# Attention in a two-layer fp32 model: two PSUM banks for the transposed probabilities, four places for their copies, the products with values a step later, and the sums in two full banks

## The chip, the core and the metric

One core of a Trainium2 chip runs the whole program. The metric is device time in microseconds (us), the median of three timed executions. The engines are PE (TensorE, the matrix engine, with its weight loads as PEld), DVE (VectorE), ACT (ScalarE), POOL (GpSimd) and SP, the engine that issues most DMAs. They run their own instruction streams and wait for one another through semaphores. Matrix products land in PSUM, eight banks of 512 fp32 columns on 128 partitions.

## The reference

The model maps x (64 batch elements, 32 tokens, 512 features) through two layers. The first is a state-space convolution along the tokens and a feed-forward with low-rank experts; the second is attention over a paged cache and such a feed-forward again. The change lies in the attention:

```python
q, k, v = x @ Wq.T, x @ Wk.T, x @ Wv.T          # 32 query heads, 8 key heads, D = 128
q, k = rope(rmsnorm(q)), rope(rmsnorm(k))
k_all = concat([k_cache[block_table], k])        # 512 cached keys + 32 own
v_all = concat([v_cache[block_table], v])
scores = where(valid, q @ k_all.T / sqrt(128), -1e30)
o = softmax(scores) @ v_all                      # 4 query heads share one key head
return o @ Wo.T
```

Each batch element has 16 cached pages of 32 keys. The 32 tokens of the 4 query heads that share a key head make 128 rows, so one unit of work is one key head of one element: 128 rows of scores over 544 keys. There are 64 x 8 = 512 units.

## The kernel before

`attention` (line 974) is a software pipeline written out by hand. `turns` (line 671) makes one loop step for each unit and calls `step` with a predicate `live(k)`: the work under `live(k)` in step u belongs to unit u - k. Each engine has its own `step` and runs its parts in the order in which they are written. One turn of the loop is 16 steps, two batch elements; a group is four units, the half of an element that fills a set of sums.

On PE, a step holds:

- under `live(4)` (line 1122) the scores: six fp32r matmuls of 272 columns, two for each of three split products. They go into banks 0 to 3 in turn.
- under `live(6)` (line 1131) four transposes of the probabilities `pr` into the one bank `ps_w` (bank 4). They wait for `s_e` (ACT has made these probabilities) and for `s_pt >= m` (ACT has copied the unit before out of the bank).
- once for each group, under `live(7)` (lines 1139 and 1141), the transposes of the probabilities of the own keys (`pr_new`) and, every second group, of the reciprocal sums `ri`. They go into the right half of bank 5 or 7.
- under `live(7)` (line 1156) four matmuls with values: `v_raw` times `pt`, ACT's copy of the transposed probabilities. They wait for `s_pt`, at k == 2 also for `s_o`, at k == 0 for `s_wn`. `pt` has two places.
- once for each group, under `live(8)` (line 1164), four matmuls for the own values, each over 64 of the 128 partitions. `v_new` is block-diagonal with zeros elsewhere: head k has its 32 rows at partitions 32k to 32k + 31.

ACT copies the finished sums to `ot` (lines 1248 to 1252), copies `ps_w` to `pt` (line 1260), copies `pt_new` and `rt`, takes the exponentials with their sums (line 1273), and once an element rounds the queries (line 1278). DVE splits the keys into a high part (line 1202) and a low part (line 1205), adds the mask and takes the row maxima (line 1212), and splits the queries (line 1226).

What sets the loads: when PE has ended the second group's own values of element b (`s_nw`), POOL copies the next row numbers (line 1086) and gathers the values of b + 2 by four indirect DMAs (line 1080). SP at the same signal loads the own values of b + 2 (line 1038), stores element b (lines 1044 and 1046), and then issues the queries (line 1019) and the 17 key loads (lines 1030 and 1033) of b + 3. DVE's first key split of an element (line 1202 at g == 0) waits for all 17.

Names used below: the step of an element counts 0 to 7 by PE's loop, j mod 8. Step 0 comes directly behind line 1164 of an element's second group in the kernel before, so POOL's copy falls at the start of step 0. The first key split is in DVE's step 2; its low part, in step 3, is needed by the scores of step 4.

## Time and profile before

| | |
|---|---|
| median of 3 runs | 2556.46 us (2554.64 to 2559.14) |
| profiled execution | 2546.38 us, span 2544.5 us |
| PE busy | 2437.2 us, 96% of the span |
| DVE, ACT, POOL busy | 1890.9, 1315.4, 764.1 us |
| attention | about 825 to 2080 us of the span |
| DMA | 213 GB/s over the span |

A line of the timeline gives the start, the time from first start to last end of a run of equal instructions, the engine, the line of the kernel and what is written from what. An fp32 matmul stands there as two records, a transpose as one. In brackets stands the idle time before it and what ended it. The end of a matmul is modelled and overlaps the next one, so the starts are the thing to compare. "Remote" as the releaser means that the profile ties the end of the wait to no instruction of this core.

### The profile page before, as it was taken

Reading aid. Unit: us, or ns where it says so; the run is one execution under the profiler, and the core shown is the slowest. Engines: PE = TensorE matmul, PEld = TensorE weight load, DVE = VectorE, ACT = ScalarE, POOL = GpSimd, SP = SyncE. Lnnn points to the kernel's source line nnn. Section 1 sums busy time; section 2 is a strip of 40 time slices with the busy share of each in tenths; the row PEclk is TensorE's granted clock in tenths of the full one; section 3 lists DMA queues with packets and bytes.
Section 4 is the critical chain, followed back from the end, with each engine's and each line's share of the span. In section 5 each row is a group of like instructions: output and inputs, shape, how many; then the busy total and the mean of one; then the engine's idle time right before and its main releaser. Section 6 shows DMA issues by size and latency. Waiting matters only on the chain. (4 is left out here: it accounts for less than half of the span.)

```text
span 2544.5 us, 54152 instructions
## 1 busy us (share of the span) xinstructions
PE 2437.2 (96%) x16128; PEld 2136.9 (84%) x16128; DVE 1890.9 (74%) x3300; ACT 1315.4 (52%) x3824; POOL 764.1 (30%) x740
## 2 busy tenths in 40 slices
PE   5999999999989999999999999999999989999999
PEld 4777877787767899999999999999999977777767
DVE  7568999999951777777777777777777766566652
ACT  2325555555532667666667666666666651111120
POOL 0235666666631122222222222222222221131120
PEclk8999999999999999999999999999999999999999
DMA  8623333333346688888888888878888886756512
GB/s 313 236 88 98 96 95 95 95 111 95 95 139 205 219 287 271 284 296 276 272 289 291 275 279 291 288 268 280 292 289 273 286 265 218 231 188 221 186 49 99
DMA packets 434116, 542.35 MB, mean 213 GB/s; under 512 B 36980, under 2 KB 350100, under 8 KB 429460
## 3 DMA queue, kind: packets, MB, share of 16 engines
q1 hardware_dynamic: 391012, 394.37, 46.6%
q0 software_dynamic: 36864, 134.23, 16.1%
q10 hardware_dynamic: 6192, 13.13, 1.5%
q8 instruction: 28, 0.46, 0.1%
q14 instruction: 20, 0.16, 0.0%
HBM read 440.59 MB, written 101.01 MB: 213 GB/s over the span
## 5 line engine op out<-in xcount | busy, mean ns | idle before, releaser
L1212 DVE CUSTOM_DVE_ANT_0 at_sm<-ps,at_mask 128x544 f32<-128x544 f32 x512 | 369.1, 721 | 297.4 <-PE ps L1122 199.9
L1156 PE MATMUL ps<-at_pt,at_v_raw 128*128 128x128 f32 x4096 | 542.0, 275 | 2.8 <-issue 2.8
L1156 PEld LDWEIGHTS ps<-at_pt,at_v_raw 128*128 128x128 f32 x4096 | 498.5, 192 | 3.0 <-issue 3.0
L1260 ACT ACTIVATE at_pt<-ps 128x512 f32<-128x512 f32 x512 | 304.1, 594 | 324.7 <-PE ps L1131 215.9
L1273 ACT ACTIVATE at_pr<-at_sm,at_nm 128x544 f32<-128x544 f32 x512 | 382.9, 748 | 59.7 <-DVE at_nm L1212 48.2
L895 POOL TENSOR_TENSOR pr_m<-pr_qn,tb 128x256 f32<-128x256 f32 x320 | 331.9, 1057 | 250.6 <-DVE pr_qn L864 235.5
L1131 PE MATMUL ps<-constants,at_pr 128*128 128x128 f32 x2048 | 310.7, 274 | 33.0 <-ACT at_pt L1260 31.0
L732 PE MATMUL ps<-pr_hi,xh 128*128 (+1 forms) x768 | 318.4, 415 | 7.9 <-DVE pr_qn L864 5.5
L1205 DVE TENSOR_TENSOR at_k_lo<-shared,at_k_hi 128x1088 fp32r<-128x1088 f32 x256 | 325.8, 1273 | 0.0
L1080 POOL DMA_INDIRECT at_v_raw<-v_cache,at_idx x256 | 287.1, 1122 | 113.4 <-issue 62.6
L733 PE MATMUL ps<-pr_lo,xh 128*128 (+1 forms) x768 | 305.1, 397 | 0.0
L734 PE MATMUL ps<-pr_hi,xl 128*128 (+1 forms) x768 | 303.5, 395 | 0.0
L822 ACT ACTIVATE pr_sq<-ps 128x128 f32<-128x128 f32 x640 | 168.5, 278 | 226.9 <-DVE f_a L857 223.8
L1086 POOL COPY at_idx<-at_rows 128x4 uint32 (+1 forms) x64 | 11.9, 186 | 901.4 <-PE ps L1164 823.7
L1131 PEld LDWEIGHTS ps<-constants,at_pr 128*128 128x128 f32 x2048 | 238.6, 141 | 49.3 <-issue 25.9
L1122 PE MATMUL ps<-at_k_hi,at_q_hi 128*128 128x272 f32 x1024 | 257.6, 333 | 2.1 <-ACT pr_stage L846 2.1
L1415 PE MATMUL ps<-op_o_hi,op_w_hi 128*128 128x512 f32 x512 | 205.6, 402 | 8.2 <-DVE op_o_lo L1380 8.2
L1122 PE MATMUL ps<-at_k_hi,at_q_lo 128*128 128x272 f32 x1024 | 212.6, 289 | 0.0
L1122 PE MATMUL ps<-at_k_lo,at_q_hi 128*128 128x272 f32 x1024 | 211.6, 288 | 0.0
L1364 ACT ACTIVATE op_o_hi<-o_raw 128x2048 fp32r<-128x2048 f32 x32 | 61.2, 1915 | 288.7 <-PE ps L1417 288.7
L1417 PE MATMUL ps<-op_o_hi,op_w_lo 128*128 128x512 f32 x512 | 205.5, 401 | 0.0
L1416 PE MATMUL ps<-op_o_lo,op_w_hi 128*128 128x512 f32 x512 | 204.8, 400 | 0.0
(237 smaller groups left out, 4374.5 us busy)
## 6 DMA issues: line engine op xcount, KB each, us to landing
shared<-k_t SPq DMA_DIRECT2D x1024, 128.0 KB
qk_t<-pr_stage SPq DMA_DIRECT2D x160, 256.0 KB
shared<-qk_t SPq DMA_DIRECT2D x64, 512.0 KB, 7.6
o_t<-at_ot SPq DMA_DIRECT2D x64, 512.0 KB
o_raw<-o_t SPq DMA_DIRECT2D x32, 1024.0 KB, 6.0
shared<-ri_d SPq DMA_DIRECT2D x32, 1024.0 KB, 8.1
f_w<-wqkv SPq DMA_DIRECT2D x12, 1024.0 KB, 6.1
s_k_in<-k_cache SPq DMA_DIRECT2D x16, 512.0 KB, 7.4
```

The lines of the kernel that those rows point to most:

```text
L732: e.matmul(out, xh[:, k, cols], hi, start=(k == 0), stop=False)
L733: e.matmul(out, xh[:, k, cols], lo, start=False, stop=False)
L734: last = e.matmul(out, xl[:, k, cols], hi, start=False, stop=(k == KB - 1))
L895: ins = e.tensor_tensor(heads(m2[:, q, :])[:, :, a], heads(qn[:, q, :])[:, :, b], table(tb, i, j - 3, a), ALU.mult)
L1080: e.indirect_dma_start(out=v_raw[:, q, c, :], out_offset=None, in_=dram["v_cache"], in_offset=bass.IndirectOffsetOnAxis(ap=idx[:, q, c:c + ...
L1122: last = e.matmul(ps[:, 2 * r + h, 0:W], a[:, q, mine], b[:, w, g % 2, h * W:(h + 1) * W], start=first, stop=end)
L1131: last = e.transpose(ps_w[:, c * P:(c + 1) * P], pr[:, w, k, c * P:(c + 1) * P], ident)
L1156: last = e.matmul(sums(w, k), v_raw[:, q, c, g * D:(g + 1) * D], pt[:, r, c * P:(c + 1) * P], start=(k % 2 == 0 and c == 0), stop=False, s ...
L1205: e.tensor_tensor(two(k_lo), raw, two(k_hi).bitcast(F32), ALU.subtract).then_inc(s_lo, 1)
L1212: e.tensor_tensor_reduce(out=halves(sm[:, r, :]), in0=ps[:, 2 * r:2 * r + 2, 0:W], in1=halves(mask[:, q, :]), scale=-SC, scalar=3e38, op0= ...
L1260: e.activation(pt[:, r, :], ps_w, ACT.Copy).then_inc(s_pt, 1)
L1273: e.activation(pr[:, w, k, :], sm[:, r, :], ACT.Exp, bias=nm[:, at], scale=-1.0, accum_out=su[:, at]).then_inc(s_e, 1)
```

## The change

The transposed probabilities go to bank 4 and bank 7 in turn, and the transposes wait for the copy of the unit before the last (`s_pt >= m - 1`). `pt` has four places and lies in another part of SBUF. The products with values come under `live(8)`, one step later; the own values under `live(9)`, the copy of the sums under `live(10)`. The four sums of a group take one full bank, 5 or 6; the transposed `pr_new` and `ri` go into the bank of the other group's sums, before these begin, and wait for `s_o` there. The own values are four matmuls over all 128 partitions, with one signal in place of two. The sums of each group are copied by one activation. The lead of the loop is 12 steps in place of 11.

```diff
         place("gap2", [P, 256])
-        self.pt = place("pt", [P, 2, LK])
+        place("gap4", [P, 2 * LK])
         place("gap3", [P, 32])
...
+        pt = sb("pt", [P, 4, LK])
...
-        ps_w = ps[:, 4, :]
-        turned = lambda w: ps[:, 7 - 2 * w, 2 * P:4 * P]
-        sums = lambda w, k: ps[:, 6 if k >= 2 else 5 + 2 * w, k % 2 * P:(k % 2 + 1) * P]
-
-        steps = lambda e, step: turns(e, B * UB, PER, 11, step)
+        ps_w = lambda r: ps[:, 4 + 3 * r, :]
+        turned = lambda w: ps[:, 6 - w, 0:2 * P]
+        sums = lambda w, k: ps[:, 5 + w, k * P:(k + 1) * P]
+
+        steps = lambda e, step: turns(e, B * UB, PER, 12, step)
...
-                    e.wait_ge(s_nw, (b + 1) * 4)
+                    e.wait_ge(s_nw, (b + 1) * 2)
                     load_v(b + 2, q)
                     store(b, q)
...
-                    wait_apart(e, s_passed[0], (s_nw, (b + 1) * 4))
+                    wait_apart(e, s_passed[0], (s_nw, (b + 1) * 2))
                     indices(b + 2, q)
...
                     e.wait_ge(s_e, m + 1)
-                    wait(e, s_pt, m)
+                    wait(e, s_pt, m - 1)
                     for c in range(KC):
-                        last = e.transpose(ps_w[:, c * P:(c + 1) * P], pr[:, w, k, c * P:(c + 1) * P], ident)
+                        last = e.transpose(ps_w(jj % 2)[:, c * P:(c + 1) * P], pr[:, w, k, c * P:(c + 1) * P], ident)
                     last.then_inc(s_c, 1)
                 if live(7) and (j - 7) % QU == QU - 1:
                     jj = j - 7
                     w = (jj // QU) % 2
                     n = jj // QU
+                    e.wait_ge(s_o, i * 4 + n + 1)
                     if w == 1:
...
-                if live(7):
-                    m, jj = u - 7, j - 7
-                    g, q, r, k, w = jj % UB, (jj // UB) % 2, jj % 2, jj % QU, (jj // QU) % 2
+                if live(8):
+                    m, jj = u - 8, j - 8
+                    g, q, k, w = jj % UB, (jj // UB) % 2, jj % QU, (jj // QU) % 2
...
-                    if k == 2:
-                        e.wait_ge(s_o, i * 4 + jj // QU + 1)
                     e.wait_ge(s_pt, m + 1)
                     for c in range(KC):
-                        last = e.matmul(sums(w, k), v_raw[:, q, c, g * D:(g + 1) * D], pt[:, r, c * P:(c + 1) * P],
-                                        start=(k % 2 == 0 and c == 0), stop=False, skip_group_check=True)
-                if live(8) and (j - 8) % QU == QU - 1:
-                    jj = j - 8
+                        e.matmul(sums(w, k), v_raw[:, q, c, g * D:(g + 1) * D], pt[:, jj % 4, c * P:(c + 1) * P],
+                                 start=(k == 0 and c == 0), stop=False, skip_group_check=True)
+                if live(9) and (j - 9) % QU == QU - 1:
+                    jj = j - 9
                     g, q, w = jj % UB, (jj // UB) % 2, (jj // QU) % 2
                     e.wait_ge(s_wn, i * 4 + jj // QU + 1)
-                    for k in (0, 2, 1, 3):
-                        rows = slice(k // 2 * 2 * S, (k // 2 + 1) * 2 * S)
-                        last = e.matmul(sums(w, k), v_new[rows, q, g // QU, k * D:(k + 1) * D], pt_new[rows, w, :],
-                                        start=False, stop=(k % 2 == 1), skip_group_check=True)
-                        if k % 2 == 1:
-                            last.then_inc(s_nw, 1)
+                    for k in range(QU):
+                        last = e.matmul(sums(w, k), v_new[:, q, g // QU, k * D:(k + 1) * D], pt_new[:, w, :],
+                                        start=False, stop=(k == QU - 1), skip_group_check=True)
+                    last.then_inc(s_nw, 1)
...
-                if live(9) and (j - 9) % QU == QU - 1:
-                    jj = j - 9
+                if live(10) and (j - 10) % QU == QU - 1:
+                    jj = j - 10
...
-                    e.wait_ge(s_nw, i * 8 + jj // QU * 2 + 2)
-                    if t == 0:
-                        e.activation(ot[:, q, 0:4 * P].rearrange("p (a x) -> p a x", a=2), ps[:, 5:7, 0:2 * P],
-                                     ACT.Copy).then_inc(s_o, 1)
-                    else:
-                        e.activation(ot[:, q, 6 * P:8 * P], ps[:, 6, 0:2 * P], ACT.Copy)
-                        e.activation(ot[:, q, 4 * P:6 * P], ps[:, 7, 0:2 * P], ACT.Copy).then_inc(s_o, 1)
+                    e.wait_ge(s_nw, i * 4 + jj // QU + 1)
+                    e.activation(ot[:, q, t * QU * P:(t + 1) * QU * P], ps[:, 5 + t, :], ACT.Copy).then_inc(s_o, 1)
...
                     e.wait_ge(s_c, m + 1)
-                    e.activation(pt[:, r, :], ps_w, ACT.Copy).then_inc(s_pt, 1)
+                    e.activation(pt[:, jj % 4, :], ps_w(jj % 2), ACT.Copy).then_inc(s_pt, 1)
```


PE in the loop, from the transposes of a step 3 on. The names are those of the code: `at_pt,at_v_raw` are products with values, `at_pt_new,at_v_new` the own values. Before:

```order
L1131 MATMUL ps<-constants,at_pr 128x128 x4
L1156 MATMUL ps<-at_pt,at_v_raw 128x128 x4
L1164 MATMUL ps<-at_pt_new,at_v_new 128x128 x4
L1115 REGISTER_ALU
L1117 REGISTER_ALU
L660 REGISTER_ALU
L1122 MATMUL ps<-at_k_hi,at_q_hi 128x272 x2
L1122 MATMUL ps<-at_k_lo,at_q_hi 128x272 x2
L1122 MATMUL ps<-at_k_hi,at_q_lo 128x272 x2
L1131 MATMUL ps<-constants,at_pr 128x128 x4
L1156 MATMUL ps<-at_pt,at_v_raw 128x128 x4
```

PE at the same place in the changed kernel, where lines 1123, 1132 and 1163 are the scores, the transposes and the own values:

```order
L1132 MATMUL ps<-constants,at_pr 128x128 x4
L1156 MATMUL ps<-at_pt,at_v_raw 128x128 x4
L1116 REGISTER_ALU
L1118 REGISTER_ALU
L660 REGISTER_ALU
L1123 MATMUL ps<-at_k_hi,at_q_hi 128x272 x2
L1123 MATMUL ps<-at_k_lo,at_q_hi 128x272 x2
L1123 MATMUL ps<-at_k_hi,at_q_lo 128x272 x2
L1132 MATMUL ps<-constants,at_pr 128x128 x4
L1156 MATMUL ps<-at_pt,at_v_raw 128x128 x4
L1163 MATMUL ps<-at_pt_new,at_v_new 128x128 x4
```

The own values have moved from the end of steps 3 and 7 to the end of steps 4 and 0, behind the next scores, transposes and products.

ACT at the turn from one element to the next, before. Here `at_ot` is the copy of the sums, `at_pt` that of the transposed probabilities, `at_pr` the exponentials and `at_q_hi` the rounded queries:

```order
L1251 ACTIVATE at_ot<-ps 128x256
L1252 ACTIVATE at_ot<-ps 128x256
L1260 ACTIVATE at_pt<-ps 128x512
L1272 REGISTER_ALU
L1273 ACTIVATE at_pr,at_su<-at_sm,at_nm 128x544
L1277 ISA
L1278 ACTIVATE at_q_hi<-shared 128x1024
L1260 ACTIVATE at_pt<-ps 128x512
```

ACT at the same place in the changed kernel:

```order
L1253 ACTIVATE at_pt<-ps 128x512
L1265 REGISTER_ALU
L1266 ACTIVATE at_pr,at_su<-at_sm,at_nm 128x544
L1270 ISA
L1271 ACTIVATE at_q_hi<-shared 128x1024
L1245 ACTIVATE at_ot<-ps 128x512
L1253 ACTIVATE at_pt<-ps 128x512
```

The copy of the sums is one activation, and it stands behind the rounding of the queries instead of ahead of the step's copy. DVE, POOL and SP have the same instructions in the same order inside the steps; the signal `s_nw` that POOL and SP wait for comes one step later.

## Rows read from the trace of the kernel before

**Rows 1.** Busy time of each engine in attention, with granted clock and DMA:

```profile
core 0: us, PE busy (x) PEld busy (x) DVE busy (x) ACT busy (x) POOL busy (x), PEclk, DMA share, GB/s
825.00:2080.00 1255.00, 1215.38 (x10434) 1166.01 (x10432) 963.86 (x1981) 857.96 (x1986) 291.64 (x311) 1.00 0.84 279
```

**Rows 2.** Who waited for whom: PE, 860 to 2080 us (total, times, longest):

```profile
PE ps L1131 <- ACT at_pt L1260: 31.0, 52, 0.7
PE ps L1131 <- issue: 2.0, 3, 0.7
```

**Rows 3.** PE in order of time, steps 2 to 5 of one element:

```profile
start us, us, engine line op out<-in xcount [idle before <-releaser]
1407.17 0.60 PE L1131 MATMUL ps<-constants,at_pr 128*128 128x128 f32 x4
...
1408.53 0.50 PE L1122 MATMUL ps<-at_k_hi,at_q_hi 128*128 128x272 f32 x2
...
1410.16 0.63 PE L1131 MATMUL ps<-constants,at_pr 128*128 128x128 f32 x4 [0.63 <-ACT at_pt L1260]
1410.62 1.06 PE L1156 MATMUL ps<-at_pt,at_v_raw 128*128 128x128 f32 x8
1411.61 0.72 PE L1164 MATMUL ps<-at_pt_new,at_v_new 64*128 64x128 f32 x8
1412.25 0.52 PE L1122 MATMUL ps<-at_k_hi,at_q_hi 128*128 128x272 f32 x2
...
1413.11 0.60 PE L1131 MATMUL ps<-constants,at_pr 128*128 128x128 f32 x4
1413.55 1.06 PE L1156 MATMUL ps<-at_pt,at_v_raw 128*128 128x128 f32 x8
1414.36 0.50 PE L1122 MATMUL ps<-at_k_hi,at_q_hi 128*128 128x272 f32 x2
```

**Rows 4.** ACT, step 2 of that element, and steps 2 and 3 two elements before:

```profile
1369.48 0.60 ACT L1260 ACTIVATE at_pt<-ps 128x512 f32<-128x512 f32 x1 [0.65 <-issue]
...
1372.72 0.60 ACT L1260 ACTIVATE at_pt<-ps 128x512 f32<-128x512 f32 x1 [1.75 <-PE ps L1131]
...
1409.41 0.60 ACT L1260 ACTIVATE at_pt<-ps 128x512 f32<-128x512 f32 x1 [2.25 <-remote]
```

**Rows 5.** DVE, step 2 and the low parts of the keys in step 3:

```profile
1408.88 0.72 DVE L1212 CUSTOM_DVE_ANT_0 at_sm<-ps,at_mask 128x544 f32<-128x544 f32 x1 [1.96 <-PE ps L1122]
...
1410.13 1.28 DVE L1205 TENSOR_TENSOR at_k_lo<-shared,at_k_hi 128x1088 fp32r<-128x1088 f32 x1
```

**Rows 6.** POOL: copies of row numbers, and one late gather:

```profile
857.33 0.18 POOL L1086 COPY at_idx<-at_rows 128x4 uint32 x1 [30.16 <-PE ps L1164]
...
1364.20 0.18 POOL L1086 COPY at_idx<-at_rows 128x4 uint32 x1 [13.25 <-PE ps L1164]
...
1368.40 0.95 POOL L1080 DMA_INDIRECT at_v_raw<-v_cache,at_idx  x1 [2.24 <-issue]
...
1382.86 0.18 POOL L1086 COPY at_idx<-at_rows 128x4 uint32 x1 [10.28 <-PE ps L1164]
...
1402.53 0.18 POOL L1086 COPY at_idx<-at_rows 128x4 uint32 x1 [13.28 <-PE ps L1164]
...
1422.01 0.19 POOL L1086 COPY at_idx<-at_rows 128x4 uint32 x1 [13.12 <-PE ps L1164]
...
2045.01 0.18 POOL L1086 COPY at_idx<-at_rows 128x4 uint32 x1 [13.09 <-PE ps L1164]
```

**Rows 7.** The stretches in which DMA runs dry (columns as rows 1):

```profile
1421.00:1422.00 1.00, 1.00 (x11) 0.87 (x11) 0.51 (x1) 0.92 (x3) 0.00 (x0) 1.00 0.07 21
...
1441.00:1442.00 1.00, 1.00 (x12) 0.88 (x9) 0.09 (x1) 0.92 (x4) 0.19 (x1) 1.00 0.33 114
```

**Rows 8.** DVE, the first key split of the next element but one:

```profile
1445.20 0.79 DVE L1202 CAST at_k_hi<-shared 128x1088 fp32r<-128x1088 f32 x1
```

**Rows 9.** PE, the first products with values:

```profile
835.99 2.05 PE L1156 MATMUL ps<-at_pt,at_v_raw 128*128 128x128 f32 x8 [2.81 <-issue]
```

More of the change, by code:

```diff
@@ L995, in attention @@
         v_raw, v_new, k_hi, k_lo, q_hi, q_lo, ot = early.v_raw, early.v_new, early.k_hi, early.k_lo, early.q_hi, early.q_lo, early.ot
-        pt, pr_new, nm, su, ri, s_in, s_qhi = early.pt, early.pr_new, early.nm, early.su, early.ri, early.s_in, early.s_qhi
+        pr_new, nm, su, ri, s_in, s_qhi = early.pr_new, early.nm, early.su, early.ri, early.s_in, early.s_qhi
         sm = sb("sm", [P, 2, NKEY])
         pr = sb("pr", [P, 2, QU, NKEY])
+        pt = sb("pt", [P, 4, LK])
         pt_new = sb("pt_new", [P, 2, P])
```

## The prediction, written before the changed kernel ran

> **What bounds the kernel now.** The first view is the busy time of attention: from 825 to 2080 us PE is busy for 1215 of 1255 us at a granted clock of 1.00, that is 2.4 GHz, DVE for 964 and ACT for 858 [rows 1]. PE sets the time there, and only what PE does or waits for counts. The second view is the waits of PE: 55 waits in this stretch, all ahead of the transposes of line 1131, 52 of them for ACT's copy `at_pt`, 0.7 us at the longest [rows 2]. The third is the timeline of PE around one of them. In step 3 the scores start at 1408.53 and the transposes at 1410.16, 1.63 us later; in step 4 the same distance is 0.86 (1412.25 to 1413.11) [rows 3]. With the slower restart (0.46 against 0.44 from the transposes to the products) a wait costs about 0.8 us.
>
> Why is the copy late? The transposes of step 2 start at 1407.17 and take 0.60, but ACT begins their copy only at 1409.41, after 2.25 us of idleness that the profile puts down to "remote" [rows 3, 4]. DVE, too, begins the maxima of step 2 at 1408.88, though their scores were done before 1407.6 [rows 5]. So once in most elements the news from PE reaches both readers about 1.7 us late. With one bank the next transposes cannot go on without that copy, and PE pays what its own 2.1 us step (1412.25 to 1414.36) does not cover.
>
> The lateness goes with the gathers. The element whose row numbers POOL copied at 1364.20 had its second gather late, at 1368.40 after 2.24 us of idleness [rows 6]; there ACT's copy of step 2 was on time (1369.48) and that of step 3 was the late one (1372.72, idle 1.75) [rows 4]. PE lost nothing: the next POOL copy came 18.66 us later (1382.86), where the mean of the 61 periods from 857.33 to 2045.01 is 19.47 [rows 6]. This element is nearly the experiment: everything that hangs on the gathers moved by about 1.9 us against PE's scores.
>
> **The change part by part.**
>
> *Two banks and one step more.* The transposes of a step now need the copy made two steps before, and the products with values use a copy that is a step older. A copy that starts 1.7 us late is then covered twice over. All 55 waits go as far as this copy is their cause. Their worth is the distance of the mean period from the clean one, 19.47 - 18.66 = 0.81 us for each of 62 periods, 50 us in all; 55 waits at 0.8 give 44, and the rest is the transposes of step 2 that start late without counting as idle. I take the first, since it is read from ends of periods.
>
> *What is late next.* The signal `s_nw` now comes behind step 0, so POOL's gathers and SP's loads move 2.1 us later against the scores. The late news (6.35 to 6.9 us after POOL's copy of 1402.53 [rows 4 to 6]) then falls on step 3. ACT has its slack. DVE begins the maxima of step 3 up to 1.8 us late and must still do a mask, a high part, the maxima of step 4 and a low part of 1.28 [rows 5] before the scores of step 6. Counting these up from 7.2 us after the copy I get 11.15 where PE wants to start at 11.0: 0.15 us in perhaps every second element. I charge 0.08 a period, 5 us in all; the bounds are 0 and, if also signals to PE are held back, 0.9 a period (the second rival).
>
> *Own values over 128 partitions.* Before, PE goes from the products at 1410.62 to the own values at 1411.61 and to the scores at 1412.25, where products without own values take 0.81 (1413.55 to 1414.36) [rows 3]. So the own values cost 0.18 before their first matmul and 0.64 for eight records, 0.82. The new ones have the shape of the products, eight records in 0.81. I take no change; the bounds are no change and +0.18 for each of 128 groups, 23 us, if the gap ahead of them is not due to their shape. The Trainium skill speaks on both sides here (TensorEngine Tiling (Array Packing), Key Properties and Theoretical Speedup): a change of tiling mode drains the engine, and two tiles of 64 rows work in parallel, up to twice as fast. By the second rule alone the pairs would take half of 0.81, and giving them up would cost 0.4 us a group, 51 us. The trace has 0.64 plus a gap of 0.18 that fits the drain: the rule's gain is nearly absent and what is left of it pays for the drain.
>
> *The copies of the sums.* One activation of 512 columns each time; ACT idles for a third of attention [rows 1] and the sums are now needed a step later, so nothing. The new wait `s_o` ahead of the transposed `pr_new` asks for a copy that ACT begins a step earlier, about 2 us ahead. Behind that wait stand the products and the next scores, so if ACT were more than 2 us behind, PE would wait here instead.
>
> *Keys and values.* They are requested 2.1 us later against the scores. DMA ran dry at about 1421.1 and 1441.4, 18.6 and 19.4 us after the POOL copies at 1402.53 and 1422.01, and the key split that needs the second batch came at 1445.20, 23.2 after its copy [rows 6 to 8]. In the new order the split comes at 23.2 - 2.1 - 0.7 (the shorter period) = 20.4. That leaves 1.0 us at the tighter element, so I charge nothing. If the cover goes, see the third rival.
>
> *Both ends.* The first products wait 2.81 us for their values at 836 us [rows 9]. One step of scores and transposes now stands ahead of them and can fill about 1 us of it: -1. The last group gets one step more to drain, whose work is the same: 0.
>
> The sum: -50 + 5 - 1 = -46 us. The profiled execution took 2546.4 (span 2544.5), which would become 2500. The three timed runs have a median of 2556.5, 10 us above it, and I carry the same saving over: **2510 us**.
>
> **Rivals.**
>
> *The gap ahead of the own values stays.* The gap of 0.18 could belong to the wait for `s_wn` that the first of these matmuls carries, not to its shape. Against it: the copy was made more than a step before. Then +23 us: 2533.
>
> *Signals to PE are held back as well.* The rows show only news from PE arriving late. If news from DVE is held too, the low part of the keys decides. It ends at about 5.4 us after POOL's copy in the new order and the scores of step 4 want to start at 6.0, where the old order gave them 0.8 more, since the own values stood between steps 3 and 4. Held until 6.9 they stall PE by 0.9 a period, as much as before: 62 x (0.81 - 0.9) = +6 us, 2562. If it hits every second element: 2535. For it: DVE's low part is the tightest supply of PE. Against it: in the shifted element nothing stalled, though there the scores of step 4 came 0.8 later.
>
> *Keys arrive late (the slower side).* SP and DMA become the bound if the 17 key loads of an element end more than about 22.5 us after POOL's copy; the split has 1.0 us to spare at 19.4, and DVE and PE together have about 2 more. They would be 3 us later than now, for example because the store and the gathers collide with the next element's loads. Each us beyond costs one us a period: at 23.0, 0.5 us of loss on the old period, 62 x 0.5 = +31, 2587. For it: a DMA share of 0.84 over attention [rows 1]. Against it: the queues run dry in every element now, for about 2 us.
>
> *The change does not do what it says:* PE's waits have the same count under another name, for example behind `s_o` or `s_e` because ACT itself is late with the exponentials. Then no change, 2556. ACT's 858 of 1255 us speaks against it.
>
> **How the numbers follow.** My forecast has 0.66, with its own range 2503 to 2518: the upper saving is 50 + 4, the lower one leaves 0.15 more a period. The gap that stays has 0.07, held signals 0.14 (two thirds of it in the milder form, still faster), late keys 0.05, no effect 0.04; 0.04 is for things that I don't see, half of them faster. Faster by over 0.2% (5 us, about what a measurement tells from nothing): 0.66 + 0.07 + 0.09 + 0.02 = 0.84. Within 0.2%: 0.08. Slower: 0.08. The range 2502 to 2537 takes in the staying gap and the milder form of held signals and leaves out about 0.18.
>
> **What would show it.** Right: no idle time of PE ahead of the transposes, POOL copies 18.7 to 18.8 us apart, ACT's late copy now in step 3 and still late, eight records of own values in about 0.81 with no gap ahead, DMA running dry less than 20.4 us after POOL's copy. Wrong: waits of PE ahead of the scores with DVE's low part as releaser (the second rival), DVE idle ahead of the first key split (the third), or a gap of 0.18 still ahead of the own values (the first). If the late news does not move with POOL's gathers but stays where it was, my account of its cause is wrong, even if the time is right: the two banks would still cover ACT, but DVE's low part in step 3 would end at 1411.41 where the scores now come at about 1410.6, and the gain would shrink to near nothing.

## The result

The changed kernel took 2522.53 us (median of 4 runs, 2520.02 to 2523.79) beside 2556.62 us of the kernel before on the same chip (4 runs, 2554.64 to 2559.14): a ratio of 0.9865, 95% interval 0.9853 to 0.9878. That is 34 us saved where 46 were forecast. The profiled execution of the changed kernel took 2522.86 us (span 2521.0), 23.5 less than the profiled one of before, which had been 10 us faster than its own timed runs.

The experiments fell on four chips, and on three of them the gain is absent: the kernel before takes 2498 us there, the changed one 2504 on the one chip of the three where it ran (chip 9), and its variants on the other two 2503 to 2505. So what has to be explained is both where the gain came from and why it comes on some chips only.

### The profile page after: what moved, and what is told of

Read it like the earlier page. It is cut to its first block and busy times, and to the rows that moved or that the text cites. A ratio compares the mean times of both kernels' runs of the same rounds, so it can differ in the third digit from the quotient of the medians.

```text
span 2521.0 us, 54056 instructions
## 1 busy us (share of the span) xinstructions
PE 2444.8 (97%) x16128; PEld 2178.7 (86%) x16128; DVE 1894.9 (75%) x3300; ACT 1312.9 (52%) x3760; POOL 756.2 (30%) x740
## 5 line engine op out<-in xcount | busy, mean ns | idle before, releaser
L1210 DVE CUSTOM_DVE_ANT_0 at_sm<-ps,at_mask 128x544 f32<-128x544 f32 x512 | 369.3, 721 | 264.8 <-PE ps L1123 252.8
L1156 PE MATMUL ps<-at_pt,at_v_raw 128*128 128x128 f32 x4096 | 540.9, 275 | 0.0
L1156 PEld LDWEIGHTS ps<-at_pt,at_v_raw 128*128 128x128 f32 x4096 | 497.8, 192 | 0.0
L1253 ACT ACTIVATE at_pt<-ps 128x512 f32<-128x512 f32 x512 | 304.2, 594 | 299.9 <-PE ps L1132 187.2
L1203 DVE TENSOR_TENSOR at_k_lo<-shared,at_k_hi 128x1088 fp32r<-128x1088 f32 x256 | 326.1, 1274 | 0.0
L1081 POOL DMA_INDIRECT at_v_raw<-v_cache,at_idx x256 | 279.0, 1090 | 113.0 <-issue 62.2
L1132 PE MATMUL ps<-constants,at_pr 128*128 128x128 f32 x2048 | 307.9, 272 | 0.0
L1087 POOL COPY at_idx<-at_rows 128x4 uint32 (+1 forms) x64 | 11.9, 186 | 884.2 <-PE ps L1163 805.7
L1123 PE MATMUL ps<-at_k_hi,at_q_hi 128*128 128x272 f32 x1024 | 255.7, 331 | 6.0 <-ACT pr_stage L846 3.7
L1132 PEld LDWEIGHTS ps<-constants,at_pr 128*128 128x128 f32 x2048 | 244.3, 141 | 1.2 <-issue 0.4
L1408 PE MATMUL ps<-op_o_hi,op_w_hi 128*128 128x512 f32 x512 | 205.4, 401 | 8.0 <-DVE op_o_lo L1373 8.0
L1123 PE MATMUL ps<-at_k_hi,at_q_lo 128*128 128x272 f32 x1024 | 212.7, 289 | 0.0
L1123 PE MATMUL ps<-at_k_lo,at_q_hi 128*128 128x272 f32 x1024 | 211.1, 287 | 0.0
```

The costliest lines, as they stand in the source:

```text
L1081: e.indirect_dma_start(out=v_raw[:, q, c, :], out_offset=None, in_=dram["v_cache"], in_offset=bass.IndirectOffsetOnAxis(ap=idx[:, q, c:c + ...
L1123: last = e.matmul(ps[:, 2 * r + h, 0:W], a[:, q, mine], b[:, w, g % 2, h * W:(h + 1) * W], start=first, stop=end)
L1132: last = e.transpose(ps_w(jj % 2)[:, c * P:(c + 1) * P], pr[:, w, k, c * P:(c + 1) * P], ident)
L1156: e.matmul(sums(w, k), v_raw[:, q, c, g * D:(g + 1) * D], pt[:, jj % 4, c * P:(c + 1) * P], start=(k == 0 and c == 0), stop=False, skip_gr ...
L1203: e.tensor_tensor(two(k_lo), raw, two(k_hi).bitcast(F32), ALU.subtract).then_inc(s_lo, 1)
L1210: e.tensor_tensor_reduce(out=halves(sm[:, r, :]), in0=ps[:, 2 * r:2 * r + 2, 0:W], in1=halves(mask[:, q, :]), scale=-SC, scalar=3e38, op0= ...
```

## The profile after

In the changed kernel's lines the scores are L1123, transposes L1132, products L1156, own values L1163, DVE's maxima L1210 (`at_sm`), mask L1216, high and low parts of the keys L1200 and L1203, ACT's copies of the transposed probabilities L1253, POOL's copy and gathers L1087 and L1081.

The busy time of attention, against [rows 1]:

```profile
825.00:2080.00 1255.00, 1240.91 (x10516) 1223.32 (x10515) 980.80 (x1991) 863.92 (x1930) 294.13 (x321) 1.00 0.84 285
```

PE is busy for 1241 us of 1255, where it was 1215, at the same granted clock of 1.00. Short delays between overlapping groups don't show in this figure, so periods and starts are read below. The waits of PE's weight loads from 860 to 2080 us (total, times, longest) answer to [rows 2]:

```profile
PEld ps L1123 <- issue: 10.1, 46, 0.3
PEld ps L1408 <- issue: 8.2, 1, 8.2
PEld ps L1132 <- issue: 0.4, 2, 0.2
PEld ps L1123 <- DVE at_k_lo L1203: 0.2, 1, 0.2
```

The 55 waits ahead of the transposes are gone. What is left stands ahead of the scores (L1123), up to 0.3 us each and named "issue" except once, where the profile names DVE's low part of the keys. (L1408 is the projection that follows attention.) The timeline of one element shows the place; ACT and DVE first, then PE:

```profile
1400.22 0.60 ACT L1253 ACTIVATE at_pt<-ps 128x512 f32<-128x512 f32 x1 [1.65 <-remote]
...
1400.35 0.72 DVE L1210 CUSTOM_DVE_ANT_0 at_sm<-ps,at_mask 128x544 f32<-128x544 f32 x1 [1.84 <-PE ps L1123]
...
1400.99 0.48 DVE L1216 TENSOR_SCALAR at_mask<-constants,at_lenf 128x512 f32<-128x512 f32 x1
1401.39 0.75 DVE L1200 CAST at_k_hi<-shared 128x1088 fp32r<-128x1088 f32 x1
1402.06 0.71 DVE L1210 CUSTOM_DVE_ANT_0 at_sm<-ps,at_mask 128x544 f32<-128x544 f32 x1
...
1402.92 1.26 DVE L1203 TENSOR_TENSOR at_k_lo<-shared,at_k_hi 128x1088 fp32r<-128x1088 f32 x1
```

```profile
1403.27 1.06 PE L1156 MATMUL ps<-at_pt,at_v_raw 128*128 128x128 f32 x8
1404.31 0.52 PE L1123 MATMUL ps<-at_k_hi,at_q_hi 128*128 128x272 f32 x2
...
1409.99 1.06 PE L1156 MATMUL ps<-at_pt,at_v_raw 128*128 128x128 f32 x8
1410.89 1.06 PE L1163 MATMUL ps<-at_pt_new,at_v_new 128*128 128x128 f32 x8
1411.70 0.49 PE L1123 MATMUL ps<-at_k_hi,at_q_hi 128*128 128x272 f32 x2
```

The late news has moved with `s_nw`, the signal that starts both POOL's gathers and SP's loads: it reaches ACT and DVE at 1400.22 and 1400.35, 7.0 and 7.2 us after POOL's copy of 1393.18, now in step 3 instead of step 2 [rows 4, 5]. PE goes straight past ACT's late copy. But DVE, which starts after 1.84 us of idleness, still does mask, high part, maxima and low part, and ends at 1404.18, and the scores of step 6 start right behind it at 1404.31. The scores come 0.81 us after the start of undisturbed products, so they could have started at 1404.08. In the last three rows the own values begin 0.90 after the products and the scores 0.81 after the own values, 1.71 in all, where it was 1.63 with the pairs of 64 rows (1410.62 to 1412.25) [rows 3].

POOL's copies, as [rows 6], are 61 periods from the first to the last:

```profile
859.42 0.19 POOL L1087 COPY at_idx<-at_rows 128x4 uint32 x1 [29.33 <-PE ps L1163]
...
1355.26 0.18 POOL L1087 COPY at_idx<-at_rows 128x4 uint32 x1 [12.94 <-PE ps L1163]
...
1359.45 1.95 POOL L1081 DMA_INDIRECT at_v_raw<-v_cache,at_idx  x1 [2.02 <-issue]
...
1374.03 0.18 POOL L1087 COPY at_idx<-at_rows 128x4 uint32 x1 [8.76 <-PE ps L1163]
...
1393.18 0.18 POOL L1087 COPY at_idx<-at_rows 128x4 uint32 x1 [12.96 <-PE ps L1163]
...
1412.20 0.19 POOL L1087 COPY at_idx<-at_rows 128x4 uint32 x1 [12.83 <-PE ps L1163]
...
2022.29 0.19 POOL L1087 COPY at_idx<-at_rows 128x4 uint32 x1 [12.82 <-PE ps L1163]
```

(2022.29 - 859.42) / 61 = 19.06 us a period instead of 19.47: 61 x 0.41 = 25 us, which accounts for the 23.5 that the profiled executions differ by. Again the element with a delayed gather (1355.26) is clean, and its period is 18.77, not 18.66. So there are two remainders: 19.06 - 18.77 = 0.29 a period of lateness that is not covered, and 18.77 - 18.66 = 0.11 that even a clean element now costs more.

## The experiments

The twelve runs fell on four chips, and "late" says whether `at_pt` or `at_sm` came late there in the trace. All ratios are against the kernel before on the same chip.

| run | chip | us, median | before, us | ratio, 95% | period, us | late |
|---|---|---|---|---|---|---|
| banks_only | 14 | 2504.23 | 2497.72 | 1.0027 (1.0017 to 1.0037) | 18.78 | no |
| one_bank | 14 | 2503.94 | 2497.72 | 1.0024 (1.0014 to 1.0033) | 18.78 | no |
| no_gathers | 14 | 2502.94 | 2497.72 | 1.0020 (1.0010 to 1.0029) | 18.78 | no |
| mask_step0 | 14 | 2503.15 | 2497.72 | 1.0025 (1.0015 to 1.0034) | 18.78 | no |
| after_again | 9 | 2503.9 | 2497.88 | 1.0025 (1.0015 to 1.0035) | 18.78 | no |
| late_gathers | 9 | 2504.01 | 2497.88 | 1.0023 (1.0014 to 1.0033) | 18.66 to 19.62 | no |
| full_rows | 9 | 2505.2 | 2497.88 | 1.0029 (1.0017 to 1.0040) | 18.78 | no |
| no_wn_wait | 9 | 2503.69 | 2497.88 | 1.0026 (1.0016 to 1.0035) | 18.78 | no |
| mask_step0_b | 8 | 2505.56 | 2543.19 | 0.9848 (0.9830 to 0.9866) | 18.78, one of 20.91 | yes |
| late_gathers_b | 8 | 2514.03 | 2543.19 | 0.9882 (0.9863 to 0.9900) | 18.66 to 19.78 | yes |
| banks_only_b | 4 | 2505.05 | 2497.89 | 1.0030 (1.0019 to 1.0042) | 18.78 | no |
| one_bank_b | 4 | 2503.28 | 2497.89 | 1.0022 (1.0011 to 1.0034) | 18.78 | no |

**Which part does it: bank or later step.** *banks_only* takes the later step back (likewise for the own values, the copies of sums and the lead of the loop), *one_bank* the second bank:

```
banks_only
-                if live(8):
-                    m, jj = u - 8, j - 8
+                if live(7):
+                    m, jj = u - 7, j - 7
...
one_bank
-        ps_w = lambda r: ps[:, 4 + 3 * r, :]
+        ps_w = lambda r: ps[:, 4, :]
...
-                    wait(e, s_pt, m - 1)
+                    wait(e, s_pt, m)
```

> The changed kernel with the products with values, the own values and the copies of the sums each a step earlier, as in the kernel before; the two banks, the four places and the full banks of sums stay. My theory (the two banks break the loop transposes, copy, next transposes; a late copy then meets only the products of the next step): the gathers sit where they were, the late news falls on step 2, the copy ends about 1410.0 on the clock of the old profile where the products of step 3 want to start at 1409.8, so 0.2 to 0.3 us of wait an element: 2517 to 2524, about the changed kernel. If the later step is what pays: PE waits about 0.8 us an element ahead of the products with ACT's copy as releaser, 2545 to 2560.

> The changed kernel with one bank for the transposed probabilities again, and the transposes waiting for the copy of the unit before; the values a step later stay. My theory: the late news now falls on step 3, ACT's copy of it ends 7.65 us after POOL's copy and the transposes of step 4 want to start at 6.7, so PE waits 1.0 us an element there and nothing in step 6: period 19.7 to 19.8, 2560 to 2568, slower than the kernel before. If the later step alone pays: 2520 to 2530 with no wait ahead of the transposes.

**Gathers and mask.** *no_gathers* leaves out the gathers inside the loop, so that elements 2 to 63 work on the cached values of the first two. *mask_step0* makes the mask three steps earlier:

```
no_gathers
-                    gather_values(q)
...
-                        e.wait_ge(s_vr[q], (i + jj // PER) * 16 * KC + 16 * KC)
+                        e.wait_ge(s_vr[q], 16 * KC)
mask_step0
-                if live(0) and j % UB == 3:
+                if live(0) and j % UB == 0:
```

> The changed kernel without the gathers of values inside the loop (elements 2 to 63 use the cached values of elements 0 and 1), POOL's copies of the row numbers stay. My theory (the late news from PE goes with the gathers): ACT's copy of step 3 and DVE's maxima of step 3 start on time, PE waits nowhere, period 18.76, 2503 to 2506. Rival (it goes with SP's loads and stores, which come at the same time): late starts stay, 2518 to 2523.

> The changed kernel with DVE's mask of the next element made in step 0 in place of step 3. My theory (what is left of PE's loss is DVE's low part of the keys in step 5, late because the maxima of step 3 start late and the mask stands behind them): the low part ends 0.4 us sooner after the late news, the scores of step 6 start 2.1 us after those of step 5, period 18.8, 2504 to 2509. Rival (the scores of step 6 wait for something else, or the loss moves on to step 5 or 7): 2518 to 2523.

All four take 2503 to 2504, with a period of 18.78, and the kernel before itself takes 2497.72 on this chip, 59 us less than on the chip of the prediction. banks_only and one_bank missed every forecast; no_gathers (2502.94) and mask_step0 (2503.15) lie within 1 us of theirs, but by luck, since the changed kernel has nothing to mend here. The waits of the four have nothing under "remote" in attention: one bank is no worse than two, and without gathers there is nothing to gain, because nothing is late. The runs tell nothing on the parts, but they show that the news of PE is not late everywhere, and that these variants of the changed kernel are 5 to 7 us slower than the kernel before where it is not.

**Is it the chip?** The changed kernel unchanged, on chip 9:

> The changed kernel as it is, beside the kernel before, on whatever chip is drawn. Two kinds of chip are known by now: on the one of the prediction the kernel before takes 2556.6 us and DVE's step 3 and ACT's turned copy of step 3 come some 1.8 us late (+7.1 behind GpSimd's copy instead of +5.24); on the one of the first four runs it takes 2497.7 us and nothing is late. Theory (late news of PE while the gathers are issued makes the whole gain; the own values over 128 partitions cost 6 us): where the kernel before takes about 2556 this one takes 2520 to 2525 with periods of 19.06; where it takes about 2498, this one takes 2502 to 2506 with periods of 18.78, slower by 0.25%. Rival (the first chip simply runs everything slower and the change gains 34 us on each): 2464 beside 2498.

The theory holds, the rival (34 us gained everywhere) is out: 2503.9 beside 2497.88. The same step 3 as above, in this trace; POOL's copy of this element stands at 1403.80:

```profile
1409.05 0.60 ACT L1253 ACTIVATE at_pt<-ps 128x512 f32<-128x512 f32 x1 [0.70 <-PE ps L1132]
...
1409.06 0.72 DVE L1210 CUSTOM_DVE_ANT_0 at_sm<-ps,at_mask 128x544 f32<-128x544 f32 x1
```

Both come 5.25 us after POOL's copy instead of 7.0 to 7.3. POOL's four gathers of this element start and last the same, to 0.01 us, as those of the element of 1412.20 on the other chip. One rival stays: none of the numbered chips was drawn at two times, and that of the prediction has no number on record, so what is called a chip here may be its state at that time.

**The 6 us.** *full_rows* is the kernel before with only its own values over 128 partitions; *no_wn_wait* is the changed kernel without the wait that the own values carry:

```
full_rows (against before)
-                        rows = slice(k // 2 * 2 * S, (k // 2 + 1) * 2 * S)
-                        last = e.matmul(sums(w, k), v_new[rows, ...], pt_new[rows, w, :],
+                        last = e.matmul(sums(w, k), v_new[:, ...], pt_new[:, w, :],
no_wn_wait (against after)
-                    e.wait_ge(s_wn, i * 4 + jj // QU + 1)
+                    if not live(8):
+                        e.wait_ge(s_wn, i * 4 + jj // QU + 1)
```

> The kernel before, with its four matmuls of own values a group over all 128 partitions instead of pairs over 64 each; banks, steps and order stay. Theory (this part of the change costs 0.05 to 0.08 a group, 0.12 a period, 128 groups in all): 6 to 8 us slower than the kernel before where nothing is late, 2503 to 2506 beside 2498, periods 18.78. On a chip with late news 0 to 8 us slower, since PE waits in each period anyway: 2557 to 2565 beside 2556. Rival (the 6 us come of the products standing a step later or of the second bank): no difference, ratio 1.000.

> The changed kernel without PE's own wait ahead of the own values (the copy of the turned own probabilities is guaranteed there by a wait that stands earlier; it stays where it does not). Theory (the gap of 0.09 between products and own values, and the 0.18 between own values and scores in the kernel before, is a drain of PE between the two forms, not the price of a wait instruction): no difference from the changed kernel, period 18.78 or 19.06 as on that chip, within 1 us of it. Rival (the wait instruction at a change of semaphores costs the 0.09): 0.05 to 0.09 less for each of 128 groups, 6 to 12 us less than the changed kernel, which brings it to the kernel before on a chip without late news.

full_rows takes 7.3 us more than before (4 to 10 by its interval), as forecast, so this one edit is enough for the whole loss. PE in its trace:

```profile
1409.93 1.06 PE L1156 MATMUL ps<-at_pt,at_v_raw 128*128 128x128 f32 x8
1410.83 1.06 PE L1163 MATMUL ps<-at_pt_new,at_v_new 128*128 128x128 f32 x8
1411.64 0.50 PE L1122 MATMUL ps<-at_k_hi,at_q_hi 128*128 128x272 f32 x2
```

Again 0.90 + 0.81 = 1.71 from the products to the scores. Asked in windows so narrow that each row begins with the first record still running in it, the same trace gives the last record of the products, the last of the own values and the first of the scores:

```profile
1410.72 0.28 PE L1156 MATMUL ps<-at_pt,at_v_raw 128*128 128x128 f32 x1
...
1411.61 0.28 PE L1163 MATMUL ps<-at_pt_new,at_v_new 128*128 128x128 f32 x1
1411.64 0.37 PE L1122 MATMUL ps<-at_k_hi,at_q_hi 128*128 128x272 f32 x1
```

Full records start 0.11 us apart, seven steps in 0.78 to 0.79 (1410.83 to 1411.61, 1409.93 to 1410.72). The first of the own values follows the last product by the same 0.11, so there is no gap ahead of them. Only the step to the scores is short, 0.03. That is why products followed by scores take 0.81 (seven steps of 0.11 and 0.03) while eight more records put in between add eight steps, 0.90.

In late_gathers, with the pairs, the distance is as in the kernel before:

```profile
1407.18 1.06 PE L1156 MATMUL ps<-at_pt,at_v_raw 128*128 128x128 f32 x8
1408.17 0.71 PE L1164 MATMUL ps<-at_pt_new,at_v_new 64*128 64x128 f32 x8
1408.82 0.52 PE L1122 MATMUL ps<-at_k_hi,at_q_hi 128*128 128x272 f32 x2
```

1.64. The difference of 0.07, twice a period, is 8.5 us for 61 periods (7 by the periods themselves: 61 x (18.78 - 18.66)). The kernel before, in windows as narrow, shows what the pairs do: its last product and then the starts within the own values of [rows 3]:

```profile
1411.40 0.28 PE L1156 MATMUL ps<-at_pt,at_v_raw 128*128 128x128 f32 x1
...
1411.61 0.49 PE L1164 MATMUL ps<-at_pt_new,at_v_new 64*128 64x128 f32 x4
...
1411.82 0.39 PE L1164 MATMUL ps<-at_pt_new,at_v_new 64*128 64x128 f32 x4
...
1411.93 0.39 PE L1164 MATMUL ps<-at_pt_new,at_v_new 64*128 64x128 f32 x4
...
1412.04 0.28 PE L1164 MATMUL ps<-at_pt_new,at_v_new 64*128 64x128 f32 x2
```

The eight records start two at a time, in four pairs (1411.61, 1411.82, 1411.93, 1412.04). Once they run, a pair takes the 0.11 us of one full record. But the first pair comes 0.21 after the last product instead of 0.11, the second 0.21 after the first, and the scores (1412.25) 0.21 after the last pair instead of 0.03. So the pairs run at twice the speed inside and give most of it back at their two ends: 0.85 from the last product to the scores, against 0.11 + 0.78 + 0.03 = 0.92 with full rows.

And without the wait (no_wn_wait) PE shows:

```profile
1408.67 1.06 PE L1156 MATMUL ps<-at_pt,at_v_raw 128*128 128x128 f32 x8
1409.56 1.06 PE L1164 MATMUL ps<-at_pt_new,at_v_new 128*128 128x128 f32 x8
```

0.89, and its time is 2503.69 beside the changed kernel's 2503.9: no difference, as forecast. The 0.90 is eight records of 0.11, and there was no gap that a wait could have made. The expectation's own reason, that 0.09 of it is a drain between two forms, is wrong too: in the changed kernel products and own values have one form.

**Gathers later, on a chip without and one with late news.** *late_gathers* is the kernel before whose POOL also waits for the transposes of the third unit of the next element:

```
-                    wait_apart(e, s_passed[0], (s_nw, (b + 1) * 4))
+                    wait_apart(e, s_passed[0], (s_nw, (b + 1) * 4), (s_c, b * UB + 11))
```

> The kernel before, with one more condition on GpSimd: its copy of indices, and so the four gathers of an element, also waits for the transposes of unit 3 of the next element (about 1.3 us later than now). Theory (the gathers' time against step 3 sets the late news of PE; the two elements with late gathers have a clean period of 18.66): on a chip with late news nearly all periods are 18.66 to 18.80 and the kernel takes 2500 to 2515 beside 2556. Rival A (late news belongs to a place in PE's program, not to the gathers): no change, 2550 to 2557, with PE's wait ahead of the transposes where it was. Rival B (the late news moves along with the gathers, to a later step): PE's wait stays at 0.7 to 0.9 but stands a step later, 2545 to 2557. On a chip without late news all three say the same as the kernel before, 2495 to 2500, and the trace then shows the periods of the kernel before there, 18.66.

> The kernel before with its gathers 1.3 us later, again, in the hope of a chip with late news. Theory (the gathers' time sets which step's news is late): where the kernel before takes about 2556, PE's wait ahead of the transposes of step 2 goes or moves; the periods drop to 18.66 to 18.9 outside of those in which values land late (8 us in all on the chip of the run before), 2506 to 2530. Rival (the place is fixed by PE's program or by other DMAs): 2556 to 2566, the wait of 0.7 stays at step 2. Where the kernel before takes about 2498: 2501 to 2506 once more.

On chip 9 the periods are 18.66 to 18.69 except where the gathered values come too late for PE (19.62 at the worst); those cost the 6 us, and "the same as before" was wrong by them. The clean period of the kernel before is confirmed there. POOL's copies in this trace:

```profile
1363.90 0.18 POOL L1086 COPY at_idx<-at_rows 128x4 uint32 x1 [9.98 <-PE ps L1131]
...
1382.59 0.18 POOL L1086 COPY at_idx<-at_rows 128x4 uint32 x1 [11.65 <-PE ps L1131]
...
1401.25 0.19 POOL L1086 COPY at_idx<-at_rows 128x4 uint32 x1 [11.64 <-PE ps L1131]
```

Chip 8 has late news: the kernel before takes 2543.19. Delaying the gathers by 1.3 us alone brings it to 2514.03. SP's loads and stores, which hang on the same signal, stay where they were. One element of that trace, POOL's copy at 1408.37:

```profile
1413.92 0.60 ACT L1260 ACTIVATE at_pt<-ps 128x512 f32<-128x512 f32 x1 [2.26 <-remote]
...
1415.80 0.72 DVE L1212 CUSTOM_DVE_ANT_0 at_sm<-ps,at_mask 128x544 f32<-128x544 f32 x1 [0.62 <-remote]
```

```profile
1413.03 0.50 PE L1122 MATMUL ps<-at_k_hi,at_q_hi 128*128 128x272 f32 x2
...
1414.57 0.66 PE L1131 MATMUL ps<-constants,at_pr 128*128 128x128 f32 x4 [0.55 <-issue]
```

The news is still late, 5.55 and 7.43 us after the copy. DVE's longest now falls a step later, on the maxima of step 3. ACT's does not move: this is still the copy of step 2, 0.89 us after the start of the scores of step 3 (1413.03), where it was 0.88 in the kernel before (1408.53 to 1409.41), and PE's transposes of step 3 stall for it as they did [rows 3, 4]. So it is in each second element, 29 of 59; their periods are 18.8 to 19.8, with late values in some. In 28 of the other 30 ACT's copy of step 3 is 0.3 late, PE loses nothing, and the period is 18.66; in the last two, whose second gather is late as in [rows 6], both copies are on time. Neither forecast came whole. The time is the theory's (2506 to 2530), and the rival, a wait in every element (2556 to 2566), is out. But in half of the elements the late copy keeps its place in PE's program, so the time of the gathers does not alone set it. SP's loads, whose time this edit left alone, remain a rival, and no_gathers, which was meant to tell the two apart, never ran on a chip with late news.

**The mask, on the chip with late news.**

> The changed kernel with the mask of an element made in step 0 instead of step 3, again, in the hope of a chip with late news. Theory (with late news at step 3, DVE's backlog there is what makes the scores of step 6 start 0.27 late in each element; taking the mask, 0.4 us, out of it closes that): where the kernel before takes about 2556, this one takes 2504 to 2510, 12 to 18 us below the changed kernel's 2522.5 (0.980 to 0.983 of before), period near 18.8. Rival (the backlog is not the mask's, scores of step 6 come late by the late news itself): 2520 to 2525, ratio 0.986. Where the kernel before takes about 2498: 2502 to 2505 once more, ratio 1.0025, and nothing is told apart.

2505.56, as the theory said. The news is late in every element, as in the changed kernel; the element with POOL's copy at 1386.10, DVE and then PE:

```profile
1393.18 0.73 DVE L1210 CUSTOM_DVE_ANT_0 at_sm<-ps,at_mask 128x544 f32<-128x544 f32 x1 [1.75 <-PE ps L1123]
...
1395.36 1.26 DVE L1203 TENSOR_TENSOR at_k_lo<-shared,at_k_hi 128x1088 fp32r<-128x1088 f32 x1
```

```profile
1396.19 1.06 PE L1156 MATMUL ps<-at_pt,at_v_raw 128*128 128x128 f32 x8
1397.01 0.50 PE L1123 MATMUL ps<-at_k_hi,at_q_hi 128*128 128x272 f32 x2
```

The low part now ends at 1396.62, before the products do, and the scores of step 6 follow after 0.82, 10.91 after the copy. All periods but one are 18.76 to 18.79. The kernel comes within 2.4 us of its own time on chip 14, while the kernel before takes 45 more on chip 8 than there. It is the fastest of the versions that ran on chips with late news; on chip 14 it is 0.25% behind the kernel before. It was not timed beside the changed kernel on one chip with late news, so the 17 us between them are only worked out from the periods of two traces, 61 x (19.06 - 18.78). The news is also a little less late on chip 8: the maxima of step 3 start 7.16 us after the copy in the mean, against 7.23 in the changed kernel's trace, where 0.1 less of lateness goes with a period shorter by 0.11. By that, an estimate, some 12 of the 17 us are the mask's.

**The parts once more.** The last two runs were meant for such a chip and fell on one without:

> The changed kernel with its products and own values a step earlier, as before; two banks for the turned probabilities stay. For a chip with late news (the kernel before takes 2540 to 2560): in the traces with it, the turned copy of step 3 starts at +7.0 behind GpSimd's copy and ends at +7.6, while these products would start at +7.1. Theory (the later step is what lets PE pass over the late copy; the second bank alone moves PE's wait from the transposes to the products): a wait of 0.5 to 0.7 a period ahead of products for ACT, periods 19.3 to 19.5, 2535 to 2550, ratio 0.993 to 1.003. Rival (the second bank alone is enough, since the lateness does not come back to PE): 2505 to 2525. On a chip without late news: 2502 to 2506 beside 2498 once more.

> The changed kernel with one bank for the turned probabilities (PE's transposes wait for the copy of the unit before); products and own values a step later stay. For a chip with late news: the transposes behind the late copy would start at +6.7, the copy ends at +7.6. Theory (the second bank is needed as well): a wait of 0.9 to 1.1 a period ahead of the transposes for ACT, periods 19.7 to 19.9, 2555 to 2570, ratio 1.000 to 1.010. Rival A (the later step alone does it): 2505 to 2525. Rival B (with the wait the late news lands in another step, as it did in the kernel before, where PE waited 0.7 in each second element or so): 2530 to 2550. On a chip without late news: 2502 to 2506 beside 2498 once more.

2505.05 and 2503.28 beside 2497.89, periods 18.78. Whether the second bank alone, the later step alone or only both together hide the late news was not shown.

## Why the prediction was right, and where it was off

The measured 2522.5 lies in the wide range (2502 to 2537) and outside the forecast's own range (2503 to 2518). The mechanism, PE's waits for the late copy, held; two terms of the sum were too small.

*The 55 waits and their worth (-50).* Right. They are gone, and the clean period of 18.66 is the old kernel's undisturbed one: late_gathers shows it on a chip without late news, and 61 x (19.47 - 18.66) = 49 us is the distance between the profiled execution of before (2546.4) and the 2497.8 that it takes on such chips.

*The late news goes with the gathers.* Right for this change, since `s_nw` moves gathers and loads together, and the news came late one step later. In the elements whose second gather is late it is moved (1364.20 before) or absent (1355.26 after). But as a cause it was only half borne out: with the gathers alone delayed, ACT's late copy kept its place in each second element (late_gathers_b), and on three of the four chips of the experiments the same gathers delay nothing. What makes the news late is open. The gain is the late news hidden, and the forecast holds where there is any. Forecast and measurement fell on one such chip; on the others its sign would have been wrong.

*The leftover of DVE (+5).* The mechanism and the place were right, and mask_step0_b shows it: in the changed kernel's trace the scores of step 6 start 0.13 us behind the end of the low part in nearly every element, and with the mask moved they no longer wait. This is the largest miss of size. The chain was counted to 11.15 after the copy and ends in fact at 11.0, with the scores at 11.13 (1404.31). But PE wants to start at 10.90, not 11.0, as the clean element shows (1355.26 to the scores of 1366.16), and it happens in every element, not in every second:

```profile
1366.16 0.50 PE L1123 MATMUL ps<-at_k_hi,at_q_hi 128*128 128x272 f32 x2
```

In elements like that of 1412.20 it is 0.4 late. Over the 60 elements the scores of step 6 are 0.24 late in the mean; with small delays of steps 3 to 5 the period loses 0.29 instead of 0.08: 18 us instead of 5. The own range of the forecast allowed for 0.15 more; 0.21 came.

*Own values (0).* Off by 0.11 a period, 7 us. "No gap ahead" was right. The price was wrong: 0.81 is the distance from products to scores, whose last step is only 0.03, and eight records more cost 8 x 0.11 = 0.90. Set against the 0.82 of the pairs that is 0.07 to 0.08 a group. Rival one (a gap of 0.18 stays, 23 us, because of the wait for `s_wn`) did not come; no_wn_wait shows nothing to gain from that wait. The Trainium skill says that a change of tiling mode drains the engine, and that two tiles of 64 rows work in parallel, up to twice as fast (TensorEngine Tiling (Array Packing), Key Properties and Theoretical Speedup). The trace agrees with both: a pair of records takes 0.11 us where one full record does, and the lost time at the two ends (0.10 ahead, 0.10 behind the first pair, 0.18 ahead of the scores) stands only around the change of shape. The prediction's reading that "the rule's gain is nearly absent" was wrong: the gain is there, and what stands around the changes of mode takes it back.

*The start (-1).* Cannot be told. The wait of 2.81 ahead of the first products [rows 9] is gone in the changed kernel's trace, but POOL's first copy is 2.1 us later than before (859.42 against 857.33 [rows 6]), the step by which it was moved. One and the same kernel has that copy at 853.90 in banks_only and at 857.89 in banks_only_b, so 1 us does not show there.

*Keys.* Right: the split that needs the second batch comes 20.5 us after its copy, as worked out, and DVE does not wait for it (1432.74, no idle time ahead; copy at 1412.20):

```profile
1432.74 0.75 DVE L1200 CAST at_k_hi<-shared 128x1088 fp32r<-128x1088 f32 x1
```

DMA runs dry about 19 us after the copy (a share of 0.22 from 1431 to 1432), less than the 20.4 asked for. The other rivals did not occur: the scores of step 4 are not stalled, DVE does not wait for keys, and no wait came under another name.

*The sum.* On the profiled executions: 61 x (-0.81 + 0.29 + 0.11) = -25 (measured -23.5). On the timed ones the kernel before loses 2556.6 - 2497.8 = 59 to late news, the changed one 2522.5 - 2503.9 = 19, and the own values cost 6: -59 + 19 + 6 = -34. That the 59 and the 19 are late news and nothing else of the chip is shown for the profiled executions only, by their periods. Carrying the same saving over from the profiled to the timed runs was a weak step: they differ by 10 us, and these are probably more late news (the timed runs of before left no trace), so that the timed runs had more to save. On the profiled executions the forecast of -46 was off by 22, on the timed ones by 12; the 10 us between the two are luck. The forecast's own range was also cut short by a slip: 0.15 more for each of 62 periods is 9 us, 2519 and not 2518.

## What to carry to other kernels

Idleness of an engine that the profile puts down to "remote", behind work that was long done, can depend on the chip as well as on the program: before building on it, run the kernel before on several chips. Slack between producer and reader (here a second bank and a consumer a step later, not told apart) hid such lateness though its cause stayed unknown, but what was left of it fell on the next chain with no slack: list for each engine what it must do between the late point and PE's next need, and move out of it what has no due time there (the mask, 0.5 us of DVE's time an element, was worth an estimated 12 to 17 us). And price matmuls that are put in or reshaped from the starts of single records and from the steps at both ends, not from the distance to the next group: that distance can hold a step that is paid once, however many records there are.

## What the runs showed of the hardware

- The same program, one core, takes 2497.7 to 2497.9 us on chips 14, 9 and 4, 2543.2 on chip 8 and 2556.6 on that of the prediction, all at a granted clock of 0.99 over the span. In the traces of the two slower ones PE's news reach ACT and DVE up to 2.1 us late, at one or two places in an element, in the others never. Why is open, and so is whether it is the chip or its state at the time.
- The amount can differ between executions: on the chip of the prediction 2546.4 us profiled and 2554.6 to 2559.1 timed, on chip 8 2538.7 to 2547.7 in seven timed executions, against 2495.6 to 2500.6 in 31 on chip 14.
- Records of a full 128-row fp32 matmul of 128 columns start 0.11 us apart, and the step from the last of them to the scores is 0.03. Pairs of records of 64 rows start two at a time, 0.11 us apart, but with 0.21 ahead of the first pair, 0.21 behind it and 0.21 ahead of the scores. For eight records the pairs are the faster by 0.07 to 0.08 us.
- A wait that PE carries for a semaphore long reached cost nothing that shows: 2503.69 us without it, 2503.9 with it.
